# A sandwich of attention and a mixture of experts in float32 on one core: V's projection with weights stationary and turned back, and new strings of turns

## The reference, cut to what matters

```python
x = L0_attn_x                                   # 8 batches, 512 tokens, 512 wide
x = x + _layernorm(attn(_layernorm(x)))         # 16 query heads, 4 key/value heads, rope, causal
x = x + _layernorm(ffn(_layernorm(x)))          # 2 shared experts, 16 routed, top 2
...
q = x @ Wq.T + bq
k = x @ Wk.T + bk
v = x @ Wv.T + bv                               # 512 tokens x 128 values in each batch
...
y = softmax(q k^T / scale, causal) @ v ;  return y @ Wo.T + bo
```

## Time and profile before

| | us |
|---|---|
| median of 3 runs | 1582.25 |
| lowest, highest | 1580.59, 1585.57 |
| the profiled execution's own run | 1585.65 |
| its span | 1583.9 |

### The profile page before, as it was taken

One profiled execution on the slowest core, in us unless ns is written; L12 is line 12 of the kernel. 1 busy time (PEld: TensorE's weight loads), 2 busy tenths in 40 slices (PEclk: granted clock), 3 DMA queues, 4 the chain that ended last, 5 costly groups with the idle time before them and its releaser, 6 DMA issues. The chain is left out here.

```text
span 1583.9 us, 24989 instructions
## 1 busy us (share of the span) xinstructions
PE 1442.1 (91%) x7066; PEld 1001.6 (63%) x7067; DVE 1061.7 (67%) x2119; ACT 983.1 (62%) x2423; POOL 549.0 (35%) x782
## 2 busy tenths in 40 slices
PE   5599999999999999997698979999999999999996
PEld 4364656656575665654476768777777677676774
DVE  4576777777877777774546665387777777773466
ACT  3588787777878777777433011277777777774333
POOL 2112233323323332321212124135656556562024
PEclk9688999989899898987799989999999999999998
DMA  5444566656555664644535333458776766654755
GB/s 167 61 91 66 119 150 106 157 102 128 115 123 146 108 155 82 131 105 121 191 129 186 108 118 108 164 143 237 176 205 143 179 141 136 144 95 78 299 214 207
DMA packets 103696, 222.94 MB, mean 141 GB/s; under 512 B 14228, under 2 KB 40342, under 8 KB 99672
## 3 DMA queue, kind: packets, MB, share of 16 engines
q1 hardware_dynamic: 85864, 179.92, 42.5%
q0 software_dynamic: 17696, 41.43, 13.9%
HBM read 219.20 MB, written 72.35 MB: 184 GB/s over the span
## 5 line engine op out<-in xcount | busy, mean ns | idle before, releaser
L1354 ACT ACTIVATE bank<-bank,mr 128x384 f32<-128x384 f32 (+3 forms) x512 | 254.9, 502 | 28.9 <-DVE mr L1602 28.4
L1602 DVE TENSOR_REDUCE mr<-bank 128x1 f32<-128x512 f32 (+3 forms) x352 | 214.3, 636 | 82.3 <-PE bank L2236 81.5
L1371 ACT ACTIVATE P<-bank 128x512 f32<-128x512 f32 x320 | 181.3, 596 | 82.1 <-PE bank L2250 80.6
L2165 PE MATMUL bank<-cut,xg 128*128 128x512 f32 x632 | 204.5, 405 | 2.6 <-DVE cut L1984 2.6
L1984 DVE TENSOR_TENSOR cut<-ring,cut 128x512 fp32r<-128x512 f32 x316 | 197.4, 687 | 8.3 <-ACT cut L1483 3.9
L2234 PE MATMUL bank<-Ks,Qs 96*128 96x384 f32 (+3 forms) x512 | 164.6, 390 | 37.2 <-ACT P L1371 17.2
L2165 PE MATMUL bank<-xt,ws 128*128 128x512 f32 x768 | 184.0, 398 | 0.8 <-DVE hb L1734 0.8
L1483 ACT ACTIVATE cut<-ring 128x512 fp32r x316 | 173.7, 620 | 5.0 <-issue 3.7
L2048 POOL TENSOR_SCALAR_AFFINE_SELECT P<-P 128x256 f32<-128x256 f32 (+1 forms) x192 | 94.4, 496 | 217.5 <-ACT P L1371 214.1
L2165 PEld LDWEIGHTS bank<-xt,ws 128*128 128x128 f32 x768 | 146.6, 192 | 33.3 <-issue 1.4
L2148 POOL DMA_INDIRECT z_scratch<-wst,pl x79 | 128.4, 1625 | 105.9 <-ACT wst L1504 86.3
(11 more groups left out here) (252 smaller groups left out, 2637.5 us busy)
## 6 DMA issues: line engine op xcount, KB each, us to landing
ring<-in_w SPq DMA_DIRECT2D x79, 1024.0 KB
ring<-in_w SPq DMA_DIRECT2D x79, 512.0 KB
Qs<-st SPq DMA_DIRECT2D x192, 128.0 KB, 5.0
xt<-xt_scratch SPq DMA_DIRECT2D x32, 512.0 KB, 6.4
xt_scratch<-xt SPq DMA_DIRECT2D x30, 512.0 KB, 3.0
xin<-in_x SPq DMA_DIRECT2D x8, 1024.0 KB, 6.8
rd<-rt_scratch SPq DMA_DIRECT2D x64, 128.0 KB, 3.7
xf<-x_scratch SPq DMA_DIRECT2D x8, 1024.0 KB, 9.4
```

What stands on the lines that cost most here:

```text
L1354: m = e.activation(ps[:, o * k:o * k + k], ps[:, o * k:o * k + k], ACT.Exp, scale=-1.0, bias=mr[:, G % 2, c:c + 1], accum_out=se[:, G % 2, ...
L1371: e.activation(Pt[:, p, :], bank[PA.bank[step]][:, :], ACT.Exp, scale=-1.0).then_inc(s_exp, 1)
L1602: e.tensor_reduce(mr[:, G % 2, 0:16].rearrange("p (h i) -> p h i", i=4)[:, h:h + n, i:i + 1], bank[PA.bank["max", b, p, j]][:, 0:n * k].re ...
L2165: m = e.matmul(ps, lhs(a_, k), rhs(b_, k), start=first and k == 0 and j == 0, stop=last and k == n - 1 and j == 2)
```

## The change

V is now computed as K is: the weights are stationary, `xT` moves with 512 columns, 12 matmuls in a batch. ACT writes the sum with its bias (one number for each partition, `bv_s` is now 128x1) into the fourth part of `xin` (`vsave`), PE turns it back with four transposes into the same bank (`vturn`), and ACT copies it to `Vs` as before. Since `xin` is now in use until `vturn` has read it, the load of the next x is issued after it. The preparation of the bias in the opening goes away, and with it the step `halves("bv")`. The strings `FIRST` and `SECOND` are new, with the same number of letters of each kind. In `LATER`, `x1` goes from 10 to 12, `xn` from 2 to 3, `rbc` from 31 to 35, `xtlo` from 4 to none, and `wload` is new with 32.

```diff
-FIRST = ("httthmkkmvhmkmkmvkhkhtvtmktkkmmkhhmtkmmkttmkkkmhtvmhkmkhkvhhhhktmtkktktvmkthvmmktmhtkmkk"
+FIRST = ("mmhhktktkmhktmkmkhvvhtmtthkkvkmkkmkttmmkkmmthkvhhtkmkhvhmkhkhvmthtmkkktmtvtkhkmkthtmkmmk"
...
-LATER = {"x1": 10, "xn": 2, "xtlo": 4, "rbc": 31}
+LATER = {"x1": 12, "xn": 3, "rbc": 35, "wload": 32}
...
-        if b + 1 < B:
-            P.add("xload", b + 1)
...
-        yield
+        P.add("vsave", b)
+        yield
+        P.add("vturn", b)
         P.add("vev", b)
         freed("v", b, 0)
+        if b + 1 < B:
+            P.add("xload", b + 1)
         yield
...
                     w.wait_ge(xT_pe, 4 * b)
+                    w.wait_ge(v_pe, 2 * b)
                     e.dma_start(xin[:, :, :], x[b].rearrange("(i p) d -> p i d", p=128)).then_inc(d_x, 16)
...
+                elif kind == "vsave":
+                    b, = a
+                    w.wait_ge(v_pe, 2 * b + 1)
+                    w.wait_ge(ld[6], 16)
+                    e.activation(xin[:, 3, :], bank[PA.bank["v", b, 3]][:, :], ACT.Identity, bias=bv_s[:, 0:1]).then_inc(v_act, 1)
...
-                    products(ps, 4, lambda a_, k: xT[:, a_, k, tk], lambda a_, k: wv_s[:, a_, k, :], last=False)
-                    m = e.matmul(ps, ones[:, :], bv_s[:, :], start=False, stop=True)
+                    m = products(bank[PA.bank[step]][:, :], 1, lambda a_, _: wv_s[:, a_, i, :], lambda a_, _: xT[:, a_, i, :],
+                                 first=i == 0, last=i == 3)
                     if i == 3:
                         m.then_inc(v_pe, 1)
+                elif kind == "vturn":
+                    b, = a
+                    ps = bank[PA.bank["v", b, 3]]
+                    w.wait_ge(v_act, 2 * b + 1)
+                    for i in range(4):
+                        m = e.transpose(ps[:, i * 128:(i + 1) * 128], xin[:, 3, i * 128:(i + 1) * 128], ident[:, :])
+                    m.then_inc(v_pe, 1)
```

More of the change, by code:

```diff
@@ L125 @@
 NEXT = ("kmmmmkkmmkkmmkmkmmmmmkkmmkkkmkkkmkmkmmkkmmmmkkmkmmmmkmkkmmkmmkmkkmkkkkmmk")
-FIRST = ("httthmkkmvhmkmkmvkhkhtvtmktkkmmkhhmtkmmkttmkkkmhtvmhkmkhkvhhhhktmtkktktvmkthvmmktmhtkmkk"
-         "mhmmtkhkhtmhkthmtkhmhkhhtkvtmtkthkhkh")
-SECOND = ("hmhthmktmkthmkttmtttkkmthkkmmmtmhthmttmmtmkhthkmthhktmhkkmkmmkmkhmkhmhttmkmtktkmthkhkhmm"
-          "hkhhmkhkkmhkthkmtkkhtkkkhkhkkttkhkk")
+FIRST = ("mmhhktktkmhktmkmkhvvhtmtthkkvkmkkmkttmmkkmmthkvhhtkmkhvhmkhkhvmthtmkkktmtvtkhkmkthtmkmmk"
+         "kmhmmhtkhthhkmkkkhvhktmkhtkhtmhtmthth")
+SECOND = ("mhhkmkttmtmtthktmthhkmtktkmtmmmtmhhmtmhmktkmktkmhkhhktkhmmmtkmhmthmhtktkkmhtkkmmthkkhhhm"
+          "tmmkhhkkhkhmhkmhktktkkkkkkhkkttthkk")
 EIGHTH = ("khhmkmhhhkhkkmhmtmmhthhtkhkhkmkhtmthkhtmkmhmmhmmkmkthkkkmmkkththtmhkhkkhtkmmtmhththkhtth"
@@ L438, in early @@
                 yield
-    merge(OPEN, "rhkv", {"r": rows(0), "h": halves("wk", "wq", "wv", "bv"), "k": chain(keys(0), proj(0, 0)), "v": vals(0)})
+    merge(OPEN, "rhkv", {"r": rows(0), "h": halves("wk", "wq", "wv"), "k": chain(keys(0), proj(0, 0)), "v": vals(0)})
     P.add("qmove", 0, 0, 0)
@@ L756, in program @@
             bk_s = sb("bk_s", [128, 1])
-            bv_s = sb("bv_s", [128, 128], F32R)
+            bv_s = sb("bv_s", [128, 1])
             bst = sb("bst", [128, 4, 6])
@@ L925, in bank_free @@
             if was[0] == "v":
-                w.wait_ge(v_act, was[1] + 1)
+                w.wait_ge(v_act, 2 * was[1] + 2)
             elif was[0] == "k":
@@ L1028, in program @@
         staged = {"wv": pf[:, 0:512], "wk": pf[:, 512:1024], "wq": flat[:, 0:2048], "wo": flat[:, 2048:4096], "wa": pf[:, 1024:1024 + 4 * E]}
-        bv_a, bv_q, bo_a, bo_q = (flat[0:2, c:c + n] for c, n in ((4096, 128), (4224, 128), (4352, 512), (4864, 512)))
+        bo_a, bo_q = (flat[0:2, c:c + 512] for c in (4352, 4864))
         row_ = yn[0:2, 2, 1, 1:3, :].rearrange("p a b -> p (a b)")
@@ L1066, in _ @@
                 e.dma_start(staged[name], src).then_inc(ld[wload_of[name][0]], 16)
-            e.dma_start(bv_a, bv).then_inc(ld[6], 16)
+            e.dma_start(bv_s[:, :], bv).then_inc(ld[6], 16)
             for name, src in (("wo", wo), ("wa", wa)):
@@ L1300, in bias @@
                 w.wait_ge(load, 16)
-                if before:
-                    w.wait_ge(act_ld, before)
+                w.wait_ge(act_ld, before)
                 e.activation(row, a_, ACT.Copy).then_inc(act_ld, 1)
                 w.wait_ge(dve_ld, minus)
-                w.wait_ge(pad_dve, 2)
+                w.wait_ge(pad_dve, 1)
                 e.activation(dst[0:2, :], q, ACT.Copy).then_inc(act_ld, 1)
-                w.wait_ge(act_ld, before + 2 if before else 5)
+                w.wait_ge(act_ld, before + 2)
                 e.activation(dst[0:1, :], row[0:1, :], ACT.Copy).then_inc(act_ld, 1)
@@ L1377, in _ @@
                     name, = a
[L1378 to L1381, removed]
+                    if name == "bo":
+                        bias(bo_s, bo_a, bo_q, 512, ld[7], SPLITS["wa"][0], SPLITS["bo"][1])
                     else:
@@ L1439, in _ @@
             w.wait_ge(d_b, 48)
-            w.wait_ge(pad_dve, 5)
+            w.wait_ge(pad_dve, 4)
             e.activation(b2_s[:, :], wst[0:80, 1536:2048], ACT.Copy).then_inc(b_act, 1)
@@ L1527, in _ @@
             w.wait_ge(dve_const, 1)
-            w.wait_ge(pad_dve, 3)
+            w.wait_ge(pad_dve, 2)
             def rope_first(pa, ra, ba, tab_, n, waits_for):
@@ L1636, in _ @@
                     name, = a
[L1637 to L1641, removed]
+                    if name == "bo":
+                        w.wait_ge(act_ld, SPLITS["wa"][0] + 1)
                         e.tensor_tensor(bo_q, bo_a, row_, ALU.subtract).then_inc(dve_ld, 1)
@@ L2186, in _ @@
                     b, i = a
-                    ps = bank[PA.bank[step]][:, i * 128:(i + 1) * 128]
-                    tk = slice(i * 128, (i + 1) * 128)
                     if i == 0:
@@ L2254, in _ @@
                     n, last = 2 * p + qh, kc == 2 * qh + 1
-                    w.wait_ge(v_act, b + 1)
+                    w.wait_ge(v_act, 2 * b + 2)
                     tiles = [("s", b, p, qh, kc, t) for t in range(len(score_tiles(qh, kc)))]
@@ L2447 @@
         "wq": chunks(wq.T), "bq": bq.T, "wk": chunks(wk.T), "bk": bk,
-        "wv": chunks(a[A + "Wv"].T), "bv": two(a[A + "bv"]), "wo": chunks(wo), "bo": two(a[A + "bo"]),
+        "wv": chunks(a[A + "Wv"].T), "bv": a[A + "bv"].reshape(128, 1), "wo": chunks(wo), "bo": two(a[A + "bo"]),
         "wa": chunks(a[S + "wa"]),
```

13 lines of the change are left out of this document (6 added, 7 removed).

## The result

| | before | after |
|---|---|---|
| median of 4 runs, us | 1582.49 | 1566.20 |
| lowest, highest | 1580.59, 1585.57 | 1564.71, 1569.49 |
| span of the profiled execution | 1583.9 | 1563.0 |

What follows compares the result with a forecast made beforehand. PE, busy 91% of the span, was taken as the bound around V. From the profiled 1583.9 us, 17.2 (V) and 2 (weights) off and 1 (opening) on make 18.2 less; from the median 1582.25 that gives 1564 us, range 1552 to 1576.

Steps and rivals of the forecast that it cites:

- The sum: Whole kernel: 17.2 us less for V, 2 less for the weights, 1 more in the opening; 18.2 us less.
- V's term: V's product on PE: 2.4 us saved in a batch, 17.2 us over the loop's seven, bounds 14.6 to 19.3.
- around V PE is full: Around V's projection PE is busy 30.00 of 30 us, so PE time taken out there should come out of the time.
- part of the gain is given back late in the batch: Rival: late in a batch DVE and ACT are full, half the gain goes, 8 us: 1572 to 1575; chance 0.17.
- The strings: New orders FIRST and SECOND of the same work: taken at 0, bounds -10 and +10 us.
- The strings' rival: The new order closes a third of PE's 30.6 us of idle time in six batches, 10 us: 1554; chance 0.20.
- The new wait: PE's transposes of V wait for ACT's copy: taken at 0, bound 1.5 us in a batch, 10 in all.
- its cover: PE work queued between V's last matmul and the transposes: scores, Q groups and a maximum, 2.7 to 3.1 us.
- the price of 1.5 us for ACT's queue: Upper bound per batch on the transposes' wait, as ACT's copy stands behind four exponentials in its queue.
- The last batch's weights: Shared weights issued later on SP, so `ymul` gets the second pair of `rd` earlier: 2 us gained, between 0 and 5.6.
- The opening: x's load directly ahead of the queries delays them, 1 us lost (0 to 3.7); the V there is worth nothing.
- The transposes and the clock: V's four transposes, 0.42 us, might lower PE's clock; the prediction expected no visible effect.

Runs made afterwards that it cites:

- v_twice: The changed kernel with each of V's matmuls done twice; 1585.83 us, ratio 1.0028 to the kernel before.
- form_alone: The changed kernel with the old strings FIRST and SECOND and the old numbers in LATER; 1573.59 us, ratio 0.9932 to the kernel before.

## Why the prediction was right, and what in it was not

- **The sum**: forecast 18.2 us less, measured 16.1 (13.9 to 18.5). The mechanism, PE's work at V's place on the path, was right: v_twice pays 2.25 to 2.59 us for 2.73 of work, and V's own work fell by 2.5 us in a batch. A slip in the sum is small: its terms give 2.4 us and it takes seven times 2.45, 17.2 for 16.8.
- **V's term**, 17.2 us for seven batches, was sized rightly as work, and not as time in the old order: a batch gained 1.69 us there, and the kernel 10.8. With the new order it nearly holds, 2.3 to 2.65 us in a batch and 15.5 in all. The step that failed is the one from "around V PE is full" to "so all of it comes out of the time". The rival "part of the gain is given back late in the batch" is what form_alone shows. Its way was not PE's idle time, which stayed at 31 us; the clock accounts for at most 2 of the 4 us of work that came back, and the rest is open.
- **The strings**, taken at 0, are worth 5.4 us on top of the form (0.9932 to 0.9898), together with the numbers in `LATER`, and nothing without it. V's term too high for the old order and the strings' too low are errors of opposite sign; that the total came out right is in this part luck.
- **The strings' rival** had them close waits. They open waits (31.1 to 36.5 us of idle time) and nearly halve the half-clock time (70 to 38 us). The prediction wanted half-clock stretches as many and as long as before; they are as many and half as long. That sign failed, and with it the step "I see no row that says which way and take 0".
- **Two more signs** missed. PE's total should have fallen by 17 to 20 us and fell by 34.5, since work outside V also took less time; and PE is busy 29.35 of 30 us around V, not 30.00.
- **The new wait**: 0 forecast, 0 found; its cover is worth 0.78 us in a batch, the copy takes 0.69 (forecast 0.7), and the price of 1.5 us for ACT's queue was too high.
- **The last batch's weights**, 2 us: `ymul`'s wait fell by more than forecast (6.73 to 1.93, of which 2.06 by the later weights), and the time by nothing that can be measured (0.9896 without the number, 0.9898 with it). That the second load carries the same number of steps stood in the program to be read; I looked only at the first load's place. It makes ACT wait 4.35 us; that this ate the term is likely and not shown.
- **The opening**: 1 us forecast, 1.4 found for the place ahead of the queries. Its V was worth nothing, as said.
- **The transposes and the clock**: the granted clock around V is 1.00 after the change too, transposes and all:

```profile
165.00:195.00 30.00, 29.35 (x151) 20.90 (x150) 24.85 (x42) 23.54 (x70) 7.48 (x13) 1.00 0.62 129
```

## What to carry to other kernels

A saving on the engine that bounds a stretch is worth its work only if the stretches behind it can use it. Here the same saving was worth 10.8 us in one order and 15.5 in another, with PE's idle time nearly unchanged by it both times. So look at the granted clock and at the cost of the unchanged work behind it, not only at the idle time. Where both a form and an order change, neither's worth is known from the sum; run each alone. And profile the same program twice before reading 2 us out of a trace: here a last batch of 140.7 us was 138.7 the second time. When a load is moved by a rule that holds for its kind, look at every load of that kind, and at what stands behind its consumer in that engine's queue.

## What was unexpected of the hardware

An order that leaves PE idle for longer (36.5 against 31.7 us in six batches) can come with more clock (0.96 against 0.93); with the old `SECOND` and the new `FIRST` it was 0.91, at 28 us of idle time. In all of them the clock falls about once in a batch, though no single wait of PE in these six batches is over 0.9 us. So the clock followed neither PE's total of idle time nor its longest wait in these orders. What in the order of work decides it was not isolated here, and the same program was given 38 us of half clock in one profile and 44 in another.
